# Counting tile ends by signs on ScalarE, a group table made there too, and radial rows gathered into three buffers, in the preparation of a four-layer graph network

## The reference

```python
edge_index = jnp.stack([src, dst])
x = x + _L0_gnn_ref(relu(layernorm(x)), src, dst)              # 3 rounds of neighbour means
x = x + _L1_gnn_ref(relu(layernorm(x)), edge_index, edge_attr_16, W1, b1, W2, b2)
x = x + _L2_gnn_ref(relu(layernorm(x)), edge_index, W_l, b_l, W_r, b_r, att, bias)
x = x + _L3_gnn_ref(relu(layernorm(x)), edge_attr_4, edge_attr_8, ..., src, dst, node_type_4)
```

## Time and profile before

| | us |
|---|---|
| median of three executions | 2127.27 (2122.56 to 2129.01) |
| the profiled execution | 2126.57 |
| its span from first to last instruction | 2124.8 |
| DVE busy | 1753.1 (83%) |
| PE busy | 1610.9 (76%) |
| ACT busy | 1103.9 (52%) |
| POOL busy | 977.8 (46%) |

### The profile page before, as it was taken

The page is one execution under the profiler, slowest core; times in us unless marked ns, Lnnn a source line. Parts: engine busy times, 40 slices in busy tenths (PEclk is TensorE's granted clock), DMA queues, the critical chain, the costliest instruction groups (busy, mean ns, idle before and its releaser), DMA issues.

```text
span 2124.8 us, 36111 instructions
## 1 busy us (share of the span) xinstructions
PE 1610.9 (76%) x8603; PEld 1273.5 (60%) x8603; DVE 1753.1 (83%) x5207; ACT 1103.9 (52%) x2865; POOL 977.8 (46%) x969
## 2 busy tenths in 40 slices
PE   4656668999998987455777777778377888788786
PEld 3222248888888974344776676677355555555555
DVE  8999988998998977787687787886767778778776
ACT  2787767888997963011423424245434444444443
POOL 4200001111221200577777777760057777777772
PEclk9887779999999998675978869789668787887878
DMA  5665668868886870343222222220021111111111
GB/s 181 197 192 162 181 196 326 308 225 292 323 305 246 327 261 29 110 109 82 71 76 70 79 73 73 75 64 1 32 70 56 54 56 55 55 55 55 55 55 48
DMA packets 168625, 280.38 MB, mean 132 GB/s; under 512 B 23985, under 2 KB 137272, under 8 KB 158578
## 3 DMA queue, kind: packets, MB, share of 16 engines
q1 hardware_dynamic: 132816, 191.61, 27.1%
q0 software_dynamic: 34368, 85.62, 13.4%
q10 hardware_dynamic: 1250, 0.86, 0.2%
HBM read 224.22 MB, written 53.79 MB: 131 GB/s over the span
## 4 chain that ended last, share of the span: by engine, by line
POOL 32%; DVE 13%; issue 12%; PE 11%; ACT 1%; DMA 1%; DVEq 0%; POOLq 0%; ACTq 0%
POOL G L750 19%; POOL AT L738 6%; POOL SCR L738 4%; PE PS L1995 2%; POOL EI L738 2%; PE PS L1996 2%; PE PS L1971 1%; DVE HOT_R L1252 1%; POOL G L738 1%; PE PS L1886 1%; DVE GROUPED_R L1267 1%; DVE GROUPED_R L1261 1%; DVE SCR L1426 1%; PE PS L1770 1%; PE PS L1947 0%
## 5 line engine op out<-in xcount | busy, mean ns | idle before, releaser
L750 POOL DMA_INDIRECT G<-table,src_idx x415 | 406.0, 978 | 167.3 <-issue 125.9
L2102 PE MATMUL PS<-SCR,OH 128*128 128x256 f32 x830 | 281.9, 504 | 107.8 <-DVE SCR L1723 104.7
L2102 PEld LDWEIGHTS PS<-SCR,OH 128*128 128x128 f32 x830 | 201.4, 252 | 160.3 <-DVE SCR L1723 120.7
L1886 PE MATMUL PS<-ALL_R 128*128 128x256 f32 (+3 forms) x2025 | 265.6, 288 | 22.8 <-DVE ALL_R L1314 8.1
L727 POOL DMA_INDIRECT HOT_R<-group_table,EI x56 | 63.3, 1130 | 467.0 <-PE PS L1850 252.3
L1971 PE MATMUL PS<-RX,OH 128*128 x830 | 178.4, 372 | 130.4 <-DVE SCR L1426 80.2
L1886 PEld LDWEIGHTS PS<-ALL_R 128*128 128x128 f32 (+1 forms) x2025 | 250.5, 189 | 25.6 <-issue 9.6
L1971 PEld LDWEIGHTS PS<-RX,OH 128*128 128x128 f32 x830 | 149.3, 248 | 160.2 <-issue 155.4
L738 POOL DMA_INDIRECT AT<-table,src_idx x208 | 213.8, 1028 | 63.4 <-issue 62.2
L957 ACT COPY SCR<-PS 128x640 f32<-128x640 f32 x83 | 57.5, 692 | 287.7 <-PE PS L2077 287.7
L1846 PE MATMUL PS<-HOT_R,GROUPED_R 128*119 128x448 f32 x776 | 181.9, 374 | 9.3 <-DVE G L1272 8.7
(11 more groups left out here) (430 smaller groups left out, 3883.2 us busy)
## 6 DMA issues: line engine op xcount, KB each, us to landing
ALL_R<-adjacency SPq DMA_DIRECT2D x72, 1600.0 KB, 7.5
adjacency<-ALL_R SPq DMA_DIRECT2D x26, 1600.0 KB, 7.6
AT<-dst_in_block SPq DMA_DIRECT2D x103, 128.0 KB
G<-table,src_idx POOLq DMA_INDIRECT x463, 2.5
AT<-table,src_idx POOLq DMA_INDIRECT x208, 2.9
table<-RX SPq DMA_DIRECT2D x10, 320.0 KB, 2.7
radial_rows<-SCR POOLq DMA_DIRECT2D x4, 512.0 KB, 5.7
SCR<-table,src_idx POOLq DMA_INDIRECT x111, 2.8
```

The lines of the kernel that those rows point to most:

```text
L750: pool.indirect_dma_start(G[:, p, q, :], None, tables[i], bass.IndirectOffsetOnAxis(ap=src_idx[:, VB * k + q:VB * k + q + 1], axis=0)).the ...
L1886: ins = pe.matmul(PS[0:m, n % 2, 0:2 * w], (adj(slot) if slot is not None else first_adj(b))(c, m), both(i % 2, c, w), start=j == 0, stop= ...
L2102: ins = pe.matmul(PS[:, q, 0:MSG], OH[:, p, q, :], view(SCR, M_AT + (p * VB + q) * MSG, [[1, MSG]]), start=True, stop=True)
```

## The change

1. **Counts by signs.** ACT computes sign(visit - 0.5 - tile end) for the 5 + 4 groups (`rank`, 391 values per instruction, straight out of PS); DVE only adds the rows up (one reduction for 5 groups, one for 4) and turns a sum of signs into a count by x 0.5 + NT/2. DVE makes the biases `half_below` in two small instructions early on.
2. **Group table on ACT**: |x - i| and relu(1 - .) right after the signs, and the store is issued by ACT. The table lies in SCR where attribute buffers 1 and 2 lie, so POOL waits for the store before its second attribute gather.
3. **POOL's two products** wait for `kinds_ready` rather than `valid_made`. In PE's fill order the four `j = 0` fills (which need only `kinds_ready`) come before the four `j = 1` fills (which need `marks_made`).
4. **Index copies** go from POOL to ACT, after pair 33 of the build.
5. **Radial rows**: three buffers; POOL gathers three, waits until their stores have landed, gathers the fourth. SP issues the stores, ahead of its first adjacency store.

```diff
-        RADIAL_IN_AT = HIGH0_AT + 4 * NSRC
+        def radial_in(g):
+            return view(SCR, HIGH0_AT + g % ATTR_RING * 8 * P, [[1, 8 * P]])
@@
-        FILLS = attr_fills(range(2)) + [(g, j) for g in range(VG) for j in range(2)] + attr_fills(range(2, VG))
+        FILLS = attr_fills(range(2)) + [(g, j) for j in range(2) for g in range(VG)] + attr_fills(range(2, VG))
@@ SP
+            for g in range(VG):
+                sp.wait_ge(s("radial_in"), 16 * max(g + 1, ATTR_RING))
+                sp.dma_start(radial_rows[g * P:(g + 1) * P, :], radial_in(g)).then_inc(s("radial_rows_stored"), 16)
@@ POOL
+                if g == 1:
+                    pool.wait_ge(s("groups_stored"), 16)
@@
-            pool.wait_ge(s("valid_made"), 1)
+            pool.wait_ge(s("kinds_ready"), 1)
@@
-            (index copies, group table, its store, and gather / wait / store / wait four times)
+            for g in range(VG):
+                at = bass.IndirectOffsetOnAxis(ap=tvi[:, g:g + 1], axis=0)
+                if g == ATTR_RING:
+                    pool.wait_ge(s("radial_rows_stored"), 16 * ATTR_RING)
+                pool.indirect_dma_start(radial_in(g), None, edge_attrs, at, element_offset=TURNED * P).then_inc(s("radial_in"), 16)
@@ ACT
+            def rank(to, at, n, source):
+                for g in range(n):
+                    ins = act.activation(to[:, g], source, ACT.Sign, bias=half_below[:, at + g:at + g + 1], scale=-1.0)
+                ins.then_inc(s("ranked"), 1)
+            act.wait_ge(s("scalars_made"), 3)
+            act.wait_ge(s("merge_spread"), 1)
+            rank(built_ranks, VG, GA, PS[:, 2, 0:NT])
+            act.wait_ge(s("ends_spread"), 1)
+            rank(ranks, 0, VG, PS[:, 0, 0:NT])
+            for c in range(4):
+                ins = act.activation(view(SCR, HIGH0_AT + c * NSRC, [[1, NSRC]]), iota_h[:, 0:NSRC], ACT.Abs, bias=bv[:, c:c + 1], scale=-1.0)
...
+            act.activation(view(SCR, HIGH0_AT, [[1, 4 * NSRC]]), view(SCR, HIGH0_AT, [[1, 4 * NSRC]]), ACT.Relu, bias=1.0, scale=-1.0).then_inc(s("groups_made"), 1)
...
+                if j == NORM_FROM + NBLK:
+                    (the two index copies)
@@ DVE
+            dve.wait_ge(s("scalars_made"), 1)
+            dve.tensor_scalar(half_below[:, 0:VG], tv[:, 0, :], 0.5, None, ALU.subtract).then_inc(s("scalars_made"), 1)
+            dve.tensor_scalar(half_below[:, VG:VG + GA], bv[:], 0.5, None, ALU.subtract).then_inc(s("scalars_made"), 1)
@@
-            dve.tensor_tensor(cmp[:, 0:GA], view(PS, 2 * 512, [[0, GA], [1, NT]]), view(bv, 0, [[1, GA], [0, NT]]), ALU.is_lt)
@@
-            dve.tensor_reduce(view(stv, 0, [[1, GA]]), cmp[:, 0:GA], AX, ALU.add)
+            dve.wait_ge(s("ranked"), 1)
+            dve.tensor_reduce(stv[:, 0, :], built_ranks, AX, ALU.add)
@@
+            done(dve.tensor_scalar(stv[:, 0, :], stv[:, 0, :], 0.5, NT / 2, ALU.mult, ALU.add))
@@
-            dve.wait_ge(s("ends_spread"), 1)
-            for g in range(VG):
-                (compare one group, L1114, and reduce it, L1115)
+            dve.wait_ge(s("ranked"), 2)
+            done(dve.tensor_reduce(tv[:, 1, :], ranks, AX, ALU.add))
+            done(dve.tensor_scalar(tv[:, 1, :], tv[:, 1, :], 0.5, NT / 2, ALU.mult, ALU.add))
@@ PE, turn_fills
                     if f == KINDS_AT:
                         pe.wait_ge(s("kinds_ready"), 1)
-                        pe.wait_ge(s("marks_made"), 1)
                         pe.wait_ge(s("keys_copied"), GA)
+                    if f == KINDS_AT + VG:
+                        pe.wait_ge(s("marks_made"), 1)
```

More of the change, by code:

```diff
@@ L322, in gnn_program @@
         assert 2 * NSRC + LA <= 1280
+        half_below = view(small, 0, [[1, VG + GA]])
+        built_ranks = view(HB, 0, [[NT, GA], [1, NT]])
+        ranks = view(HT, 0, [[NT, VG], [1, NT]])
         def attr_rows(g):
@@ L328, in gnn_program @@
         last_blocks = view(HB, 3120, [[1, NB]], 1).bitcast(I32)
-        RADIAL_IN_AT = HIGH0_AT + 4 * NSRC
-        assert ATTR_RING * TURNED * P <= 7688 and RADIAL_IN_AT + 8 * P <= 7688
+        def radial_in(g):
+            return view(SCR, HIGH0_AT + g % ATTR_RING * 8 * P, [[1, 8 * P]])
+        assert ATTR_RING * TURNED * P <= 7688 and HIGH0_AT + ATTR_RING * 8 * P <= 7688
         def id_rows(g):
@@ L705, in _ @@
             pool.wait_ge(s("fill_copied_act"), N_FILL)
[L706 to L712, removed]
             for g in range(VG):
                 at = bass.IndirectOffsetOnAxis(ap=tvi[:, g:g + 1], axis=0)
-                pool.indirect_dma_start(view(SCR, RADIAL_IN_AT, [[1, 8 * P]]), None, edge_attrs, at, element_offset=TURNED * P).then_inc(s("radial_in"), 16)
-                pool.wait_ge(s("radial_in"), 16 * (g + 1))
-                pool.dma_start(radial_rows[g * P:(g + 1) * P, :], view(SCR, RADIAL_IN_AT, [[1, 8 * P]])).then_inc(s("radial_rows_stored"), 16)
-                pool.wait_ge(s("radial_rows_stored"), 16 * (g + 1))
+                if g == ATTR_RING:
+                    pool.wait_ge(s("radial_rows_stored"), 16 * ATTR_RING)
+                pool.indirect_dma_start(radial_in(g), None, edge_attrs, at, element_offset=TURNED * P).then_inc(s("radial_in"), 16)
             pool.wait_ge(s("groups_stored"), 16)
@@ L722, in _ @@
             pool.wait_ge(s("block_summed"), FIRST)
+            pool.wait_ge(s("idx_made"), 2)
             for k in range(NB):
@@ L871, in _ @@
                     act.copy(banks(j), zeros2).then_inc(s("banks_zeroed"), 2)
+                if j == NORM_FROM + NBLK:
+                    act.copy(view(EI, 2 * VW + 3, [[VB, NB]]).bitcast(I32), view(EI, 2 * VW + 3, [[VB, NB]])).then_inc(s("idx_made"), 1)
+                    act.copy(src_idx[:], EI[:, 0, 0:NV + 1]).then_inc(s("idx_made"), 1)
                 if NORM_FROM <= j < NORM_FROM + NBLK:
@@ L1179, in _ @@
             dve.wait_ge(s("dve_step"), valid_made)
-            dve.tensor_tensor(va, id_part(1), id_part(2), ALU.not_equal).then_inc(s("valid_made"), 1)
+            done(dve.tensor_tensor(va, id_part(1), id_part(2), ALU.not_equal))
             done(dve.tensor_copy(vc, sixteenth))
@@ L1800, in turn_fills @@
                         pe.wait_ge(s("kinds_ready"), 1)
+                        pe.wait_ge(s("keys_copied"), GA)
+                    if f == KINDS_AT + VG:
                         pe.wait_ge(s("marks_made"), 1)
-                        pe.wait_ge(s("keys_copied"), GA)
                     if nth(f) >= 4:
```

8 lines of the change are left out of this document (5 added, 3 removed).

## The result

The changed kernel took 2144.36 us in the median of 5 runs (2142.25 to 2148.17), the kernel before 2127.27 (now the median of 5 runs too, 2122.56 to 2129.01). The ratio is 1.0085, 95% interval [1.0067, 1.0102]: slower by 17 us, where 5 us less was forecast. The profiled execution took 2146.62 us, its span is 2144.8.

A forecast was written before the change was run, and what follows sets the result against it. DVE, busy 249.58 of 250 us, bounds the build. Earlier counts, marks and visits, less a 1.7 us wait, sum to -5.4 us at visit 14: 2126.57 becomes 2121.2, plus 0.7 for the median, 2121.9 us (range 2115 to 2127).

The forecast's parts named there:

- DVE up to the first counts: Preparation: removing DVE's comparison saves 2.1 us, small additions cost 0.3 and 0.2, no wait for ACT; `pairs_found` shifts by -1.6.
- Rival 2: Preparation: ACT's first table load costs 1.4 us more, counts come 1.2 late; shift -4.2, 2123.1 us; chance 0.07.
- Where these shifts are cut: Preparation after the counts: POOL's gathers shift only -1.95, not -4.7; DVE's `vrow` copy -3.4, 1.3 us of saving becoming a wait.
- Marks: Preparation: L1182 no longer runs beside POOL's first product, -0.95 us; POOL's products beside the statistics cost 0 to 0.95.
- single-input rule: Preparation: DVE instructions with one SBUF input outside 2-port modes don't contend with GpSimd, so POOL's products beside the statistics cost nothing.
- The wait that takes over: Before visit 12: DVE waits about 1.7 us for ACT's square root; visit 12 starts at 57.6 instead of 62.35.
- In the build: Visits 12 and 13 without POOL's table beside them: -0.65 us; later visits keep 0.39; sum at visit 14 is -5.4 us.
- rival 3: Build: ACT and PE set the pace, not DVE; the build ends by ACT's shift, -3.0, 2124.3 us; chance 0.13.
- rival 5: Whole kernel: nothing arrives, later stages absorb the gain or their clock moves by as much, 2127 us; chance 0.06.
- rival 1: Before visit 12: DVE never waits and its whole gain arrives, shift -7.1, 2120.2 us; chance 0.14.
- Costed at nothing, radial rows: Build: radial gathers and stores hidden; SP's block 0 store lands by 86.0, ACT needs its slot at 87.0.
- Rival 4: Build: radial gathers and stores go one after the other, delaying SP's block 0 store; +8.4 us, 2135.7 us; chance 0.06.

The follow-up runs named there:

- early_fourth: Changed kernel with a fourth buffer, the fourth radial gather issued before the last fills are copied, ahead of visit 12: 2121.22 us, ratio 0.9968 to the kernel before.
- extra_once: Changed kernel with a single 128 x 1 clearing on DVE ahead of visit 44: 2121.67 us, ratio 0.9964 to the kernel before.
- pool_fourth: Changed kernel with POOL itself storing the fourth radial group, so nobody in the build depends on its gather: 2132.7 us, ratio 1.0014 to the kernel before.
- dve_waits: Changed kernel with DVE waiting ahead of visit 50 for the fourth radial gather to land: 2127.39 us, ratio 0.9994 to the kernel before.
- pool_touch: Changed kernel with POOL's small clearing of `wr1_s` moved to just ahead of the fourth radial gather: 2148.79 us, ratio 1.0086 to the kernel before.
- pool_stores_all: Run 5: changed kernel with radial rows as before, one buffer, POOL gathering, waiting, storing, waiting: 2162.12 us, ratio 1.0153 to the kernel before.
- 6: Also before_sp_stores: the kernel before, one buffer, with SyncE issuing the four radial stores ahead of the adjacency stores: 2143.71 us in one execution.
- 2: Also four_buffers: changed kernel with a fourth buffer, fourth gather right behind the third: two executions of 2124.0 and 2125.7 us, four of 2145.45 to 2152.73.
- 12: Also before_three: the kernel before with only the change's radial part, three buffers and SyncE's stores: 2136.68 us, ratio 1.0046 to the kernel before.
- 8: Changed kernel with POOL storing the third radial group itself, waiting, then gathering the fourth: one execution of 2125.70 us, four of 2146.25 to 2154.78.
- 9: Changed kernel with a 128 x 1 clearing on DVE ahead of every eighth visit from visit 32, 70 in all: 2123.39 us, ratio 0.9981.
- 13: Changed kernel with eleven more DVE tile operations of the stream's own form, ahead of visits 40, 48, ... 120: 2124.37 us, ratio 0.9973.
- 14: The run extra_once: changed kernel with one 128 x 1 clearing on DVE ahead of visit 44: 2121.67 us, ratio 0.9964 to the kernel before.
- 11: Changed kernel with POOL's group table, index copies and radial rows as before, the signs staying on ACT: 2126.31 us, ratio 0.9996 to the kernel before.
- 15: Also pool_work: changed kernel with four POOL compares into unused space between the third gather and the wait ahead of the fourth: 2125.24 us, ratio 0.9980.

## Why the prediction was wrong

Forecast 2121.9 us (2115 to 2127), measured 2144.36. By its steps:

- *DVE up to the first counts*: table load at 9.70 (forecast 9.6), signs done at 13.5 (13.4), the reduction at 13.64 (13.6) with no wait. Right. Rival 2, a dearer load, is refuted: the first sign starts 0.01 us behind the load's end, and the square root 0.02, as before.
- *Where these shifts are cut*: second group of id gathers at 24.26 (24.25), attribute gathers at 29.30 (29.25). DVE's copy of `vrow` at 22.82 (23.4), with 0.94 us of waiting instead of over 1. Right but for 0.6.
- *Marks*: 0.43 us (0.42), and the statistics that POOL's products now lie beside took 3.19 us for sixteen against 3.17. Right, at the free end of its bounds. With the single-input rule that the prediction took from the Trainium skill (SBUF — State Buffer, Who interferes with whom) the trace agrees.
- *The wait that takes over*: 1.59 us (1.7) and the root at 56.08 (56.95); visit 12 at 56.94 (57.6). Right, 0.7 us on the cautious side.
- *In the build*: visit 14 shifts by -6.1 (-5.4). With the radial rows out of the way this arrives at the end of the build, 286.69 and 285.93 in early_fourth and extra_once against 292.07, -5.4 and -6.1. Their medians, 2121.2 and 2121.7 us, lie 6.7 and 8.0 under the kernel before on the same chips. The forecast's sum for this part was right, if a little small. In these two runs DVE waits for nobody from visit 12 to the end of the build, so rival 3 (ACT and PE set the pace) is out; both intervals lie under 1, so rival 5 (nothing arrives) is out too, and rival 1 (no wait before visit 12) by the wait of 1.59 us.
- *Costed at nothing, radial rows*: this step failed. "Hidden, with 1 us to spare" reckoned the fourth gather at 1.3 us, its length in a trace in which nothing held it. It took 29.96. The step named landings as the cover and never asked whether POOL gets to issue a DMA while DVE's stream runs. Its own sign of being wrong, SyncE's first adjacency store later than 80, came true with 101.32. The 1 us to spare wasn't there either: ACT asked for its buffer at 82.80, not 87.0, so a store landed at 86.0 would have been 3 us late, and DVE's lead would have had to cover that. In extra_once, where the gather takes 3.76 us, that costs nothing measurable.
- *Rival 4* had the place (block 0's store behind SyncE's radial stores, forecast 101.0, measured 101.32) but another cause (gathers and stores one after the other), a chance of 0.06, and a price of +8.4 where +17.2 came. That the two times nearly agree is luck. Of ACT's 26.3 us DVE's lead covered 8.3 at the first stop, as reckoned (7.8), but six short waits behind it took 4.2 back, so 4.1 in all.

What the Trainium skill says on it was not weighed. Its page SBUF — State Buffer (Terms, and "SBUF: two separate sides") describes a port pair that DVE and GpSimd take by turns, exclusively, and a GpSimd queue that can't write its descriptors while DVE holds it. The runs agree in direction: POOL is kept out while DVE runs. That a port is what it lacks, no run here shows. How each held instruction ended:

| kernel | POOL instruction | took us | DVE stopped | it ended behind that by |
|---|---|---|---|---|
| changed | gather | 29.96 | 96.21 | 0.81 |
| pool_fourth | gather | 219.09 | 287.14 | 0.82 |
| dve_waits | gather | 5.94 | 73.21 | 0.81 |
| pool_touch | clearing | 29.41 | 97.12 | 0.15 |
| pool_stores_all | store | 227.22 | 286.57 | 0.12 |

The page gives ("A bandwidth-pool intuition that's wrong") about 0.115 us from DVE's end to the end of the block; the last two rows, 0.15 and 0.12, agree, and the gathers, with 0.81 or 0.82, end later. The same page makes the hold last for one DVE instruction. These runs differ from it: here it lasted over some 74 visits in the changed kernel, two instructions each and a start every 0.396 us, and over 551 in pool_fourth (218.3 us by 0.396).

**What stays open.** Why the kernel before is never held: its 83 executions on record took 2122.56 to 2136.05 us. The stream is the same, 0.3959 us per visit behind visit 20 in either. The runs rule out the engine that issued the DMA before (5, 6), the wait ahead of the gather (2, where there was none) and an idle POOL (12). They show that one program can have both outcomes (2, 8), that the one profiled execution of 8 with a first passage had the second too, and that an instruction between the tiles opens the way (9, 13, 14). In all kernels in which POOL was computing while DVE went into the stream (before, before_sp_stores, before_three, 11, 15) everything passed; in the others with a POOL instruction inside the stream it was held in all executions or most, unless DVE's pace was broken. But POOL's computing also slows DVE's first visits (15) and so shifts its stream, and no run separates the two. All of this would fit two engines that fall into step, but what they step by no trace here shows.

## What to carry to other kernels

When a POOL instruction moves into a stretch in which DVE runs back to back, price it from zero to the whole stretch, even if the trace before shows it there at 1 us, and then ask who is queued behind it. Let nothing in such a stretch depend on POOL: issue its DMAs before the stretch, or give DVE one extra instruction behind the point of issue. The best kernels here are the changed one with the fourth gather moved ahead of the stream (0.9968) or with a single 59 ns clearing in it (0.9964), each faster than both kernels. Moving the gather is the safer of the two, since why the clearing works isn't known.

## What the hardware showed that was not expected

- One POOL instruction held for 219 us, by a DVE stream with no gap and no loss of its own (no visit over 0.40 us from visit 12 on in pool_fourth).
- A clearing of 128 x 128 is held in the same way as a DMA's issue (29.41 us in pool_touch).
- One program with two times, 2124.0 to 2125.7 and 2145.5 to 2152.7 us (four_buffers); the profile of a short execution has POOL passing.
- POOL's compares slow DVE's tiles beside them: visits of 0.56 to 0.80 us for 0.396 in pool_work.
